# Linear attention with a routed feed-forward layer on one core: scores of two quads in five visits instead of six

## What is computed

```python
# attention: 16 heads of 16 features; taylor_exp(q).taylor_exp(k) is ((q.k/4 + 1)^2 + 1)/2
A = tril(einsum('bhnd,bhmd->bhnm', taylor_exp(q), taylor_exp(k)))
y = einsum('bhnm,bhme->bhne', A, v) / row sums of A
out = y @ Wo.T
# feed-forward: 8 experts of width 512, the two best per token, softmax weights
h, g = x @ W1[e], x @ W2[e]
y = (silu(h) * g) @ W3[e]          # times the token's weight, summed over its two experts
```

## Time and profile before

| | us |
|---|---|
| median of 3 runs | 641.88 (640.58 to 643.51) |
| profiled execution | 641.04 |
| its span in the trace | 639.2 |
| TensorE busy in the span | 615.2 (96%) |
| one batch of the first stage, steady | 35.04 to 35.06 |

### The profile page before, as it was taken

One profiled execution on the slowest core, in us unless ns is written; L12 is line 12 of the kernel. 1 busy time (PEld: TensorE's weight loads), 2 busy tenths in 40 slices (PEclk: granted clock), 3 DMA queues, 4 the chain that ended last, 5 costly groups with the idle time before them and its releaser, 6 DMA issues.

```text
span 639.2 us, 16670 instructions
## 1 busy us (share of the span) xinstructions
PE 615.2 (96%) x5181; PEld 475.7 (74%) x5181; DVE 449.5 (70%) x1134; ACT 348.3 (54%) x515; POOL 360.2 (56%) x453
## 2 busy tenths in 40 slices
PE   8899999999999999998999899999999999999995
PEld 8555665666666666665788788888888888888884
DVE  6866878787787776587797466667666666676663
ACT  3668878787878777775565233333333333333331
POOL 4256464637364654556157366665666666666645
PEclk9999999999999999998999999999999999999998
DMA  4753554545544444552863455656656566565553
GB/s 132 175 120 102 125 170 102 159 96 154 138 105 122 101 121 100 159 150 75 306 174 68 102 118 123 124 121 125 121 121 127 116 125 126 119 124 120 124 100 43
DMA packets 73347, 80.37 MB, mean 126 GB/s; under 512 B 12368, under 2 KB 61392, under 8 KB 73264
## 3 DMA queue, kind: packets, MB, share of 16 engines
q1 hardware_dynamic: 56144, 50.72, 30.5%
q0 software_dynamic: 16704, 28.12, 22.4%
q10 hardware_dynamic: 416, 0.46, 0.3%
HBM read 27.72 MB, written 22.95 MB: 79 GB/s over the span
## 4 chain that ended last, share of the span: by engine, by line
PE 44%; issue 24%; POOL 17%; DVE 8%; POOLq 2%; ACT 2%; DMA 1%; DVEq 0%; ACTq 0%
PE banks L1172 10%; POOL xg L545 8%; PE banks L1154 8%; PE banks L1192 7%; POOL out L571 6%; PE banks L1298 5%; PE banks L1201 4%; PE banks L1236 4%; POOL mark L557 3%; POOLq L555 2%; PE banks L1319 2%; PE banks L1221 2%; PE banks L1227 1%; ACT T L608 1%; DMA out<-yo,xw 1%
## 5 line engine op out<-in xcount | busy, mean ns | idle before, releaser
L571 POOL DMA_INDIRECT out<-yo,xw x71 | 112.6, 1586 | 101.4 <-DVE yo L1101 82.3
L536 POOL TENSOR_SCALAR_AFFINE_SELECT T<-T 128x512 f32<-128x512 f32 x128 | 80.1, 637 | 109.4 <-ACT T L614 43.0
L1298 PE MATMUL banks<-w12h,xgh 128*128 x284 | 112.9, 397 | 2.7 <-DVE xgl L1079 2.5
L1298 PE MATMUL banks<-w12l,xgh 128*128 x284 | 111.4, 392 | 0.0
L1298 PE MATMUL banks<-w12h,xgl 128*128 x284 | 111.0, 391 | 0.0
L1113 DVE TENSOR_TENSOR hs<-banks,hs 128x512 f32<-128x512 f32 x71 | 49.1, 692 | 84.2 <-PE banks L1298 79.1
L707 ACT ACTIVATE sTh<-banks 128x512 fp32r<-128x512 f32 x71 | 42.4, 599 | 92.6 <-DVE banks L1089 76.6
L545 POOL DMA_INDIRECT xg<-xs_scr,glist x71 | 72.6, 1022 | 24.5 <-issue 20.6
L1172 PE MATMUL banks<-T,vau 128*17 128x512 f32 (+3 forms) x1024 | 75.5, 435 | 0.0
L527 POOL DMA_INDIRECT xs_scr<-xb,slots x64 | 64.4, 1005 | 19.2 <-issue 12.6
L1154 PE MATMUL banks<-Q,K 32*128 32x256 f32 (+2 forms) x1024 | 69.5, 361 | 2.2 <-DMA K<-Kt 1.7
(11 more groups left out here) (186 smaller groups left out, 1246.4 us busy)
## 6 DMA issues: line engine op xcount, KB each, us to landing
hq<-hs SPq DMA_DIRECT2D x244, 64.0 KB
w12r<-w SPq DMA_DIRECT2D x16, 512.0 KB, 4.6
Q<-Q SPq DMA_DIRECT2D x126, 64.0 KB, 2.4
out<-xa SPq DMA_DIRECT2D x16, 256.0 KB, 2.3
w3r<-w SPq DMA_DIRECT2D x8, 512.0 KB, 8.3
K<-Kt SPq DMA_DIRECT2D x126, 32.0 KB
xa<-x SPq DMA_DIRECT2D x7, 512.0 KB, 4.8
xg<-xs_scr,glist POOLq DMA_INDIRECT x71
```

The costliest lines, as they stand in the source:

```text
L536: e.affine_select(out=v, in_=v, pattern=[[0, 4], [1, P]], compare_op=ALU.is_ge, fill=-1.0, base=0, channel_multiplier=-1).then_inc(s["g_mk ...
L571: e.indirect_dma_start(out, bass.IndirectOffsetOnAxis(xw[:, t % XR, NE:NE + 1].bitcast(U32), 0), yo[t % 3], None, compute_op=ALU.add).then ...
L1298: i = e.matmul(banks[:, 2 * (t % 2) + m, :], a[:, k, :], w[:, bass.ds(expert[t] * 4 + (2 * k + m), 1), :], start=(k == 0 and n == 0), stop ...
```

## The change

Two quads, an even one and the odd one behind it, now have five visits. Part 0 is as before. Part 1 holds key block 1 (384 columns) and key block 3 (now 128 wide), which together fill the bank. Part 2 exists for even quads only and holds key block 2 of both quads, 256 columns each; it waits for the moved q and k of both `h`. T1 and T2 become 4 x 512 wide, and ScalarE squares full banks in every visit. Counts of semaphores follow `group(n, part)`: five visits for two quads. The masks are still four for each quad; the two of part 2 are made in the even quad. The buffers yw move to other memory. For batches 1 to 6 the two `x` steps of the second quad move from slot b to slot a, that is, ahead of scores part 1, and `places` moves ahead of them on VectorE.

```diff
 def slot_a(n):
-    return [("C", 0, 0), ("f", 1, 6)] if n == 0 else []
+    b, qd = divmod(n, 4)
+    if n == 0:
+        return [("C", 0, 0), ("f", 1, 6)]
+    return [("x", b + 1, 0), ("x", b + 1, 1)] if qd == 1 and 0 < b < LAST else []
...
     elif qd == 1:
-        steps = [("x", b + 1, 0), ("x", b + 1, 1)] if b else [("v", 1, 0)]
+        steps = [] if b else [("v", 1, 0)]
...
+def group(n, part):
+    return 5 * (n // 2) + 3 * (n % 2) + part
...
-        T1 = r1.take("T1", 1536, F32, (4, 384))
-        T2 = r2.take("T2", 1536, F32, (4, 384))
-        yw = [r1.take("yw0", 512), r2.take("yw1", 512)]
+        T1 = r1.take("T1", 2048, F32, (4, 512))
+        T2 = r2.take("T2", 2048, F32, (4, 512))
+        ry = Region(Q1, Q1 + 1024)
+        yw = [ry.take(f"yw{u}", 512) for u in range(2)]
...
+            def masks(n):
+                b, qd = divmod(n, 4)
+                mask(n, T0[n % 2][:, :, 0:P], 0)
+                if sends_after(n, 0):
+                    send(*sends_after(n, 0))
+                mask(n, T1[:, :, 0:P], 1)
+                if sends_after(n, 1):
+                    send(*sends_after(n, 1))
+                mask(n, T1[:, :, 384:512], 1)
+                if qd == 2 and b < NBATCH - 2:
+                    root(b + 2)
+                if n % 2 == 0:
+                    mask(n, T2[:, :, 0:P], 2)
+                    mask(n, T2[:, :, 256:384], 2)
+                if sends_after(n, 3):
+                    send(*sends_after(n, 3))
...
-                    e.activation(T1[:, 2 * h:2 * h + 2, :], banks[:, 2 * h:2 * h + 2, 0:384], ACT.Square, scale=0.25,
+                    e.activation(T1[:, 2 * h:2 * h + 2, :], banks[:, 2 * h:2 * h + 2, :], ACT.Square, scale=0.25,
...
-                    e.activation(T2[:, 2 * h:2 * h + 2, :], banks[:, 2 * h:2 * h + 2, P:512], ACT.Square, scale=0.25,
+                    e.activation(T2[:, 2 * h:2 * h + 2, :], banks[:, 2 * h:2 * h + 2, :], ACT.Square, scale=0.25,
...
-                elif qd == 1 and b < LAST:
-                    places(b)
...
                 if n:
                     copy_yw(n - 1)
+                if n % 4 == 1 and n // 4 < LAST:
+                    places(n // 4)
                 for item in slot_a(n):
                     step(*item)
...
-                jobs = (((0, 0, 512),), ((1, 0, 384),), ((3, 0, 256), (2, 256, 256)))[part]
+                jobs = (((h, 0, 0, 512),), ((h, 1, 0, 384), (h, 3, 384, 128)), ((0, 2, 0, 256), (1, 2, 256, 256)))[part]
+                if part == 2:
+                    e.wait_ge(s[f"d_q{g}1"], MOVES * (b + 1))
+                    e.wait_ge(s[f"d_k{g}1"], MOVES * (b + 1))
...
-                scores(n, 2)
+                if n % 2 == 0:
+                    scores(n, 2)
                 for item in slot_c(n):
                     step(*item)
```

More of the change, by code:

```diff
@@ L528, in send, with mask @@
                                          xb[b % 2][:, blk, :], None).then_inc(s[f"d_xs{b % 2}"], 16)
-            def mask(n):
-                b, qd = divmod(n, 4)
[L532 to L539, removed]
+            def mask(n, v, part):
+                e.wait_ge(s["a_s"], 2 * group(n, part) + 2)
+                e.affine_select(out=v, in_=v, pattern=[[0, 4], [1, P]], compare_op=ALU.is_ge, fill=-1.0, base=0,
+                                channel_multiplier=-1).then_inc(s["g_mk"], 1)
+            def masks(n):
+                b, qd = divmod(n, 4)
+                mask(n, T0[n % 2][:, :, 0:P], 0)
[12 more added lines that the diff above has]
+                    send(*sends_after(n, 3))
             def gather(t):
@@ L575, in gpsimd_program @@
             for n in range(NQ):
-                mask(n)
+                masks(n)
             done(e, "G", 0, 0)
-            e.wait_ge(s["p_s"], 6 * NQ)
+            e.wait_ge(s["p_s"], 5 * NQ)
             e.wait_ge(s["d_xs0"], 512)
@@ L596, in squares0 @@
                 for h in range(2):
-                    e.wait_ge(s["p_s"], 6 * n + h + 1)
+                    e.wait_ge(s["p_s"], 2 * group(n, 0) + h + 1)
                     if n >= 2 and h == 0:
@@ L612, in squares2 @@
                 for h in range(2):
[L613 to L614 removed]
+                    e.wait_ge(s["p_s"], 2 * group(n, 2) + h + 1)
+                    e.activation(T2[:, 2 * h:2 * h + 2, :], banks[:, 2 * h:2 * h + 2, :], ACT.Square, scale=0.25,
                                  bias=1.0).then_inc(s["a_s"], 1)
@@ L1151, in scores @@
                             if j == 0 and p == 0 and r % 2 == 0 and n + part:
-                                e.wait_ge(s["a_s"], 6 * n + 2 * part + r // 2 - 1)
+                                e.wait_ge(s["a_s"], 2 * group(n, part) + r // 2 - 1)
                             rr = slice(32 * r, 32 * r + 32)
-                            i = e.matmul(banks[:, r, c0:c0 + w], K2[rr, g, h, jm * P:(jm + 1) * P], Q2[g][rr, h, p, 512 - w:512],
-                                         start=(p == 0), stop=(p == 1))
+                            i = e.matmul(banks[:, r, c0:c0 + w], K2[rr, g, hj, jm * P:(jm + 1) * P],
+                                         Q2[g][rr, hj, p, 512 - w:512], start=(p == 0), stop=(p == 1))
                             if j == len(jobs) - 1 and p == 1 and r % 2:
@@ L1167, in attend @@
                     e.wait_ge(s["c_b4"], 1)
-                for jm, w, v, mk in ((0, 512, T0[n % 2], 1), (1, 384, T1, 2), (3, 128, T2[:, :, 0:P], 3),
-                                     (2, 256, T2[:, :, P:384], 4)):
-                    e.wait_ge(s["g_mk"], 4 * n + mk)
+                mine = 256 * (n % 2)
+                for jm, w, v, mk in ((0, 512, T0[n % 2], (1, 6)), (1, 384, T1[:, :, 0:384], (2, 7)), (3, 128, T1[:, :, 384:512], (3, 8)),
+                                     (2, 256, T2[:, :, mine:mine + 256], (4, 5))):
+                    e.wait_ge(s["g_mk"], 8 * (n // 2) + mk[n % 2])
                     for r in range(4):
```

9 lines of the change are left out of this document (5 added, 4 removed).

## The result

The changed kernel takes 634.25 us (median of 4 runs, 633.86 to 635.06), the kernel before 641.75 on the same chip (4 runs): 0.9874 of it, 95% interval 0.985 to 0.9898. The forecast was 637.9 with a range from 635.0, so the direction was right and the gain, 7.5 us, was almost twice the 4.0 forecast. The profiled execution took 635.06 us (before 641.04), its span 633.3. All ratios compare fast executions; the only slow one on record, 849.08 us in experiment 5, is left out.

A forecast was written before the change was run, and what follows sets the result against it. TensorE was taken as the bound, except VectorE's chain in the last batch. Pairs -4.6, batches 1 to 6 +0.3, first batch +0.35, last batch 0: -4.0 us, from the median 641.88 to 637.9; range 635.0 to 645.0.

The forecast's parts named there:

- the price of a merged pair: Scores of two quads on TensorE: 3.78 us before, 3.45 after with part 1 at 0.72, a gain of 0.33.
- Rival 1: Key block 3 in every part 1: narrow rounds run like float32, 0.58 us more per pair, 646.3 us; chance 0.18.
- rival 2: Part 1: narrow rounds at half the price of 256-wide ones, 1.4 us more gained, 636.5 us; chance 0.12.
- Rival 4: Merged visits: the fixed 0.19 us is a wait that comes back, 2.7 us less gain, 640.6 us; chance 0.05.
- Rival 3: First quad: ScalarE's squares release banks late, 0.4 us in seven batches, 2.8 us, 640.7 us; chance 0.15.
- 0.45 us lost: Third quad: longer squares queue on ScalarE until 185.9, so the fourth quad's scores wait, 0.45 us per batch.
- at nothing: Steady batches: a stall of TensorE for a mask or a moved k, counted as zero.
- Batch 0: First batch: no gain of 0.4 from moving x, and 0.35 us lost against the pairs' saving; forecast -0.3.
- The feared wait for the moved q: Batch 0, first quad: part 2 waits for moved q of the second `h`, nothing to about 0.7 us; taken as 0.
- The last batch: VectorE's chain bounds it; later low parts against the missing part 2, between 0.15 gained and 0.35 lost; taken as 0.
- about 1.0 us later: Last batch: VectorE's chain starts about 1.0 us later, since copies of q and k stand behind longer squares.
- what the first gains passes through: Second stage: untouched, its start waits for nothing with its own date, so the first stage's gain is kept whole.

The follow-up runs named there:

- experiment 5: Changed kernel with `places` put back behind the x steps on VectorE, x staying early: 644.95 us against 642.67, ratio 1.0012.
- experiment 3: Kernel before, with key block 3 computed 128 columns wide instead of 256, still in part 2, all visits kept: 642.55 us against 642.18, ratio 1.0002.
- experiment 4: Kernel before, with T1 and T2 squared 512 wide and yw moved, TensorE's work unchanged: 646.29 us against 642.18, ratio 1.0065.
- experiment 1: Changed kernel with the x steps back in slot b and `places` back behind them: 644.93 us against 642.18, ratio 1.0033.
- experiment 6: Changed kernel with SyncE moving q and k for each `h` in turn: 634.66 us against 642.67, ratio 0.986.
- experiment 7: Changed kernel with `places` split, its first four instructions ahead of `copy_yw`, its last two behind x: 634.7 us against 642.67, ratio 0.9875.
- experiment 2: Kernel before, six visits, with the x steps in slot a and `places` ahead of them: 644.77 us against 642.18, ratio 1.0038.
- experiment 8: Kernel before with 13 filler matmuls instead of 4 in the last quad: 642.55 us against 642.67, ratio 0.9995.
- experiment 9: Changed kernel with q/k moves per `h` and `places` split: 631.18 us; also `w12_low(8)` moved later: 629.97; changed kernel again: 636.61; kernel before: 643.16.
- the best version: Changed kernel with q/k moves per `h`, `places` split and `w12_low(8)` moved behind VectorE's last-batch chain: 629.97 us, ratio 0.9798.

## Why the prediction was right or wrong

**Right.** TensorE bounds the batches 1 to 6, and the price of a merged pair is as worked out: part 1 0.72 us, so 0.33 us for each pair. The number is right, but the reason given for it (new weights load under the wide round, 0.06 us, and not under a narrow one, 0.11) isn't shown: the same reasoning gave 0.60 to 0.65 us for part 2 of experiment 3, and it took 0.66 to 0.67. Some of the agreement may be luck. Rival 1 (narrow rounds like float32) would have shown 1.0, rival 2 (half price) 0.67. The Trainium skill, "TensorE: Matmul & The Clock Gate", section Back-to-back issue gap, also gives about 81 ns for a 128-wide matmul in a stream with its weight loads. Two would be 0.16 us, an estimate from that page that the measured 0.17 agrees with; by the isolated figure, which the prediction weighed, it would be 0.11. Rival 4 (the fixed 0.19 us is a wait that comes back) fell too: behind part 1 of the fourth quad the chain goes on without a wait, and the first and second quads changed by the forecast's amounts within 0.05 us. Rival 3 put the late release into the first quad: experiment 4 has the longer squares and the first quad stays at 8.50.

**The step that failed in the batches: the third quad's queue on ScalarE.** The prediction added three delays (squares 0.17 later and 0.43 longer, squares of part 2 another 0.43) and booked "0.45 us lost" on top of the longer visit. About 0.2 came. The addition treats ScalarE as full from part 1 on. It wasn't: the earlier trace rows shows the copy of k end at 183.24 and the next squares start at 183.33, while after the change, where they follow at once, the second starts 0.12 before the first one's end; and the copy itself had waited for TensorE. Those gaps took up part of it. Counted from the start of part 1's scores, the copy of k starts 0.42 us later and the squares of part 2 end 0.67 later; the prediction had 0.60 and 1.03. What is left of the delay shows as 0.04 us in the third quad and as 0.17 in the fourth, whose scores take 0.84 us instead of 0.67. Experiment 4 has the same 0.2 us without the merge.

The other part had no term in the prediction at all: the step behind the removed visit costs less. The second group of the output projection takes 1.43 us in the chain, and before

```profile
191.46 1.63 PE banks L1236 x12
```

(the first group 1.64 before, 1.62 after). Third and fourth quads together were forecast at +0.12 us and measured at -0.31. That is 0.4 us for each batch, half from each part. That the fourth quad alone met its forecast (-0.52 for -0.50) is luck: the late squares (+0.17) and the cheaper step (-0.20) cancel in it. Batches 2, 3 and 6 keep all of it (0.95 to 1.00 gained, not 0.6). Batches 1, 4 and 5 gained 0.78, 0.55 and 0.34: there it is mostly the moved k (waits of 0.39, 0.29 and 0.40 us), a stall that the prediction counted "at nothing", that took it back.

**Batch 0** gave 1.22 us where 0.3 was forecast. The feared wait for the moved q exists, and is small: the visit takes 1.18 us instead of 0.75. But the fourth quad gained 0.78: before it had waited 0.41 us for `yw` and 0.25 for squares ahead of the third visit, and the scores behind it took 1.10 us. Without that visit the 0.25 is gone and these scores take 0.74, while the wait ahead of step t has grown to 0.72. The gain repeats: batch 0 takes 31.4 to 31.9 us in experiments 1, 5, 6 and 7, and 32.6 in experiments 2 and 8, which have six visits.

**The last batch** was forecast at 0 and gave 1.87 us. TensorE before, then after, where the busy share by stretch shows the difference:

```profile
294.30:296.60 2.30, 0.04 (x1) 0.07 (x2) 2.00 (x4) 0.41 (x1) 2.10 (x4) 1.00 0.16 61
296.50:298.60 2.10, 2.04 (x22) 1.52 (x22) 1.23 (x5) 0.00 (x0) 0.49 (x1) 0.61 0.18 66
298.60:302.00 3.40, 3.40 (x40) 1.48 (x36) 1.58 (x3) 3.30 (x5) 1.51 (x3) 0.74 0.00 0
```

```profile
290.20:293.00 2.80, 2.10 (x22) 0.68 (x20) 2.55 (x7) 2.35 (x4) 2.61 (x4) 1.00 0.27 100
293.00:296.73 3.73, 3.29 (x43) 2.52 (x35) 2.04 (x6) 0.00 (x1) 2.36 (x4) 1.00 0.13 37
```

Of the 1.87 us, 0.92 lies in VectorE's chain, which ended 30.66 us behind the batch's first scores instead of 31.58, and 0.95 behind it, where the last visit and the low clock are gone. The forecast of "about 1.0 us later" for that chain had the wrong sign: q's low part came 0.34 later, but the chain behind it was 1.26 shorter. Nearly all of this is in the lengths of VectorE's instructions, not in waits: seven of them are 0.2 to 0.5 us shorter than before (2.4 us together) and four 0.2 to 0.4 longer (1.2). Two of the seven, with GpSimd's rows of the same moment, before and then after:

```profile
293.99 0.69 DVE L955 TENSOR_TENSOR lists<-lists,part 128x128 f32<-128x128 f32 x1
294.72 0.62 DVE L956 SCALAR_TENSOR_TENSOR lists<-rown,cumt,lists 128x128 f32<-128x128 f32 x1
```

```profile
292.94 1.59 POOL L527 DMA_INDIRECT xs_scr<-xb,slots  x1 [0.30 <-issue]
294.55 0.64 POOL L536 TENSOR_SCALAR_AFFINE_SELECT T<-T 128x512 f32<-128x512 f32 x1
```

```profile
287.80 0.29 DVE L977 TENSOR_TENSOR lists<-lists,part 128x128 f32<-128x128 f32 x1
288.13 0.35 DVE L978 SCALAR_TENSOR_TENSOR lists<-rown,cumt,lists 128x128 f32<-128x128 f32 x1
```

```profile
286.59 1.77 POOL L536 DMA_INDIRECT xs_scr<-xb,slots  x1 [0.16 <-issue]
```

The same two instructions take 0.69 and 0.62 us where they meet the end of a send and a mask, 0.29 and 0.35 beside a send alone. All eleven instructions that are stretched in one of the two profiles meet a mask or the end of a send; not all that do are stretched. Which ones are hit goes with the alignment of the two engines.

It isn't a property of the change, as the other profiles show. With five visits, experiments 1, 5 and 6 (whose last batch has the changed kernel's program, but for SyncE's order in 6) end VectorE's chain 32.05, 31.58 and 31.46 us behind the first scores, against 30.66. With six visits, experiments 2, 3, 4 and 8 end it at 31.76, 31.11, 30.21 and 31.15 us, against 31.58; in experiment 2 the last batch's program is that of the kernel before. So the two kinds of kernel overlap. From the first scores to the first tile experiments 2 and 3 need 39.88 and 39.35 us where the kernel before needed 40.42: its one profile is a long one. Tile 5 begins 65.83 and 65.81 us behind them in the two profiles of the changed kernel, 67.56, 67.49 and 67.32 in experiments 1, 5 and 6, and 66.58 to 67.73 in the six-visit kernels. The 1.87 us repeat for one binary, but how much of them belongs to the change stays open. That it is the alignment was argued from these rows, not tried.

**The end.** That "what the first gains passes through" the second stage held to tile 15 (7.89 us ahead), and then 1.85 were lost by the last tile, in stalls of which I can only say where they fell. By terms: batches 1 to 6 0.9 more than forecast, batch 0 0.9, the start 0.1, the last batch 1.9, the second stage 1.9 less; together the 2.0 by which the profiled execution beat its forecast of 637.0.

The range left no room below rival 2. Nearly every bound in it was for costs. Gains of a removed visit beyond its own price (a wait ahead of it, the cheaper step behind it) had no term at all, and the one rival on that side stopped at 636.5.

## What to carry to other kernels

When work is removed from behind a wait it was covering, price the cover with it: five visits alone were 0.3% slower and the earlier x alone 0.4% slower, yet together with `places` 1.3% faster. Read the busy queue of a neighbouring engine for its gaps before adding delays along it; only what is left over after the gaps arrives. If two waits stand one behind the other, try their cures together, as each alone shows little. And before a gain is put down to a change, see how far the same stretch varies between profiles of kernels in which it has the same program.

## What was not expected of the hardware

- A 128-wide round at the head of a visit takes as long as a 256-wide one (part 2 at 0.66 to 0.67 us with either), two of them behind a wide round 0.17 us.
- The output projection's second group takes 1.43 us in the chain where it stands behind transposes, and 1.63 behind a visit of scores; the first group, behind scores in both kernels, takes 1.62 to 1.64. That the change from the row-tiled scores (a head in each quarter of the rows) to full matmuls costs this 0.2 us is the likely reading, and no run isolates it.
- Idle TensorE of 1.66 to 1.79 us was followed by a granted clock of 0.50 to 0.76 for several us in two of six batches of experiment 1 and in four of six of experiment 5, and in the others, with the same wait, by none. Idle time of 2.30 us in the last batch was followed by 0.61 and 0.74 in the kernel before, and by 1.00 in experiment 2.
- VectorE's instructions that read two tiles of SBUF (one of them can be a column of scalars) took up to 0.5 us longer when they met GpSimd's mask or the end of its send; reductions and reads of PSUM in the same chain did not. The Trainium skill, "SBUF — State Buffer", section SBUF: two separate sides, describes a port pair shared by these two engines that such instructions compete for; the rows agree in the kind of instruction that is stretched, and no run here isolates it.
- In experiments 5, 6 and the two kernels of experiment 9 with new orders ScalarE's first copy of the second stage starts about 1.7 us behind the transposes that it waits for (in the changed kernel 0.03), in the view of waits as a wait for "remote". What that is stays open, and it is what the best version would be worked on next.
